# Windowed attention with a routed feed-forward layer: score mask on two engines, gathers that add, and a queue in another order

## The reference

```python
xn = layernorm(x)
q, k, v = split(xn @ qkv_w.T)            # 32 heads of 8 channels
attn = q @ k.T * 8 ** -0.5
m = where(i - 8 <= j < i + 8, (8 - abs(i - j) / 2) / 8, 0)
attn = softmax(where(m != 0, attn * m, -inf))
s = (attn @ v) @ proj_w.T + proj_b
logits = xn @ router_w                   # 8 experts
e, score = argmax(logits), sigmoid(max(logits))
h = silu(score * xn @ gate_w[e]) * (score * xn @ up_w[e])
ffn = h @ down_w[e] + (silu(xn @ sgate_w) * (xn @ sup_w)) @ sdown_w
out = x + s * silu(ffn)
```

## Time and profile before

| | |
|---|---|
| median of 3 runs | 641.51 us |
| lowest and highest | 639.12, 642.87 us |
| profiled execution, its own time | 641.16 us |
| its span, first to last instruction | 639.3 us |
| mean granted TensorE clock | 0.97 |

### The profile page before, as it was taken

How to read it: one execution, slowest core, us unless ns; L and a number is a source line. 1 busy time by engine, 2 the same in 40 slices (tenths; PEclk the granted TensorE clock), 3 DMA queues, 4 the chain that set the end, 5 groups by cost and what they waited for, 6 DMA issues and landing times. The chain is left out here.

```text
span 639.3 us, 10599 instructions
## 1 busy us (share of the span) xinstructions
PE 562.8 (88%) x3358; PEld 484.0 (76%) x3358; DVE 404.0 (63%) x853; ACT 308.1 (48%) x762; POOL 186.8 (29%) x160
## 2 busy tenths in 40 slices
PE   2879999969879999999999999999886868789865
PEld 1657888858757899898999898898775756677754
DVE  6655746886755455455455455456688888886773
ACT  1374654557773544543544634546454543635332
POOL 6000101147861011010010110014645545532230
PEclk9899999979998999999999999999989899989997
DMA  9415532112326667666567576443133333330110
GB/s 294 133 62 190 177 122 61 57 44 96 111 87 178 174 166 223 196 184 195 165 189 223 167 218 185 134 133 107 51 98 110 102 106 105 113 109 20 43 35 23
DMA packets 107370, 82.89 MB, mean 130 GB/s; under 512 B 42292, under 2 KB 104756, under 8 KB 107316
## 3 DMA queue, kind: packets, MB, share of 16 engines
q1 hardware_dynamic: 98628, 68.72, 36.6%
q0 software_dynamic: 3072, 8.39, 4.1%
q10 hardware_dynamic: 5616, 5.11, 2.3%
HBM read 59.12 MB, written 23.07 MB: 129 GB/s over the span
## 5 line engine op out<-in xcount | busy, mean ns | idle before, releaser
L425 POOL TENSOR_TENSOR Sx<-Sx,mx 128x752 f32<-128x752 f32 x64 | 93.7, 1464 | 414.9 <-DVE mx L725 414.8
L941 PE MATMUL psV<-VB,PTs 128*128 128x132 f32 x1024 | 137.3, 288 | 43.3 <-DMA VB<-v_dram 19.0
L941 PEld LDWEIGHTS psV<-VB,PTs 128*128 128x128 f32 x1024 | 130.1, 197 | 50.8 <-issue 50.0
L468 ACT ACTIVATE Or<-psV 32x128 f32<-32x128 f32 x256 | 68.5, 268 | 151.4 <-DVE rs L755 148.9
L916 PE MATMUL psS<-kBD,qBD 128*128 128x188 f32 x512 | 104.9, 329 | 0.0
L916 PEld LDWEIGHTS psS<-kBD,qBD 128*128 128x128 f32 x512 | 87.9, 195 | 10.8 <-issue 2.0
L747 DVE STREAM_TRANSPOSE PTs<-Sx 128x512 f32<-128x512 f32 x128 | 82.9, 685 | 1.0 <-ACT Sx L498 1.0
L991 PE MATMUL psM<-xT,EB 128*128 128x128 f32 x624 | 76.4, 276 | 0.0
L718 DVE TENSOR_TENSOR Sx<-psS,cst 128x752 f32<-128x752 f32 x64 | 59.7, 933 | 26.3 <-PE psS L916 26.2
L991 PEld LDWEIGHTS psM<-xT,EB 128*128 128x128 f32 x624 | 73.9, 192 | 2.1 <-ACT qBD L487 1.3
L732 DVE SCALAR_TENSOR_TENSOR ea<-et,psM 128x256 f32<-128x256 f32 x39 | 16.4, 421 | 76.3 <-PE psM L991 47.2
(11 more groups left out here) (107 smaller groups left out, 690.6 us busy)
## 6 DMA issues: line engine op xcount, KB each, us to landing
EB<-in_L_ffn_gate_w SPq DMA_DIRECT2D x39, 256.0 KB, 3.0
EB<-in_L_ffn_up_w SPq DMA_DIRECT2D x39, 256.0 KB, 3.5
EB<-in_L_ffn_down_w SPq DMA_DIRECT2D x39, 256.0 KB, 3.1
VB<-v_dram SPq DMA_DIRECT2D x256, 32.0 KB
stage<-xs_dram SPq DMA_DIRECT2D x39, 128.0 KB, 2.2
ys_dram<-yb ACTq DMA_DIRECT2D x39, 128.0 KB, 3.1
xs_dram<-blank SPq DMA_DIRECT2D x9, 512.0 KB, 3.1
v_dram<-vS SPq DMA_DIRECT2D x8, 512.0 KB, 3.0
```

The source lines that it names most:

```text
L425: nc.gpsimd.tensor_tensor(s, s, mx[n % 3][:, :].unsqueeze(2).broadcast_to([P, 2 * G, KW]), ALU.subtract).then_inc(a_sub, 1)
L468: return nc.scalar.activation(dst, src, ACT.Copy)
L941: last = mm(psV[:, j, at:at + HS * VW], PTs[n % 2][:, k, j, i, :], VB[n % 2][:, i, k, :, VW * j:VW * j + VW], start=k == 0, stop=k == 1)
```

## The change

Three things are changed together.

1. **The mask.** In steps 0 to 7 and 18 to 63 (`masked_late`) TensorE no longer writes the mask into PSUM. The constant `band` (12 x 47 fp32 values per partition, 288 KB in all) holds the mask, and a new GpSimd operation `banded(n)` adds it to `Sx` in place, after weigh and before largest, which waits for it. In these steps VectorE's `largest(n)` moves behind `flipped(n-1)`. Steps 8 to 17 keep the order and the matmuls of before. TensorE's wait for the bf16 constants moves from step 0 to step 8.
2. **The gathers.** `combine` is gone. The indirect transfers add the expert rows straight into the shared expert's rows (`compute_op=ALU.add`). Gather(c) is issued one step before its silu, after subtract, once the shared rows are there; ScalarE's silu waits for the transfers and, from chunk 3, for the buffer `Y` to be free.
3. **SyncE's order.** For units 9 to 63 `spread_v(n-1)` stands first in step n, ahead of stores, loads, fills and the wait for the scatters.

```diff
@@ constants
+    c[:, C_BAND:C_STAY] = np.tile(c[:, C_MASK:].reshape(P, 3, 1, 2 * KW), (1, 1, KC, 1)).reshape(P, 12 * KW)
+def masked_late(n):
+    return n < BATCH or n >= E0
@@ SyncE
             for n in range(LAST + 1):
+                if BATCH < n - 1 < U:
+                    spread_v(n - 1)
                 for c in result_at(n - 1):
                     store(c)
...
-                if 0 <= n - 1 < U:
+                if 0 <= n - 1 <= BATCH:
                     spread_v(n - 1)
@@ GpSimd
+            def banded(n):
+                pool.wait_ge(a_mul, n + 1)
+                s = Sx[n % 3][:, :, :].rearrange("p (m r) k -> p m r k", r=HS)[:, :, :, 0:KW]
+                kind = 2 * KC * mask_kind(n)
+                nc.gpsimd.tensor_tensor(s, s, band[:, kind:kind + 2 * KC, :].unsqueeze(2).broadcast_to([P, 2 * KC, HS, KW]),
+                                        ALU.add).then_inc(a_add, 1)
             def gather(c):
-                b = c % 3
                 if c == 0:
                     for k in range(3):
                         pool.wait_ge(b_st[k], 16 * len(range(k, NX, 3)))
-                if c >= 3:
-                    pool.wait_ge(d_w, c - 2)
+                pool.wait_ge(f_sh, c + 1)
                 for k in range(CT):
                     t = c * CT + k
-                    pool.indirect_dma_start(Y[b][:, k * C:(k + 1) * C], None, ys_dram,
-                                            bass.IndirectOffsetOnAxis(ap=slot[:, t:t + 1], axis=0)).then_inc(d_y[b], 16)
-            def combine(c):
-                b = c % 3
-                z = shared_rows(c * CT).rearrange("p t c -> p (t c)")
-                pool.wait_ge(d_y[b], 16 * CT * (c // 3 + 1))
-                pool.wait_ge(f_sh, c + 1)
-                nc.gpsimd.tensor_tensor(z, Y[b], z, ALU.add).then_inc(d_z, 1)
+                    pool.indirect_dma_start(shared_rows(c * CT)[:, k, :], None, ys_dram,
+                                            bass.IndirectOffsetOnAxis(ap=slot[:, t:t + 1], axis=0),
+                                            compute_op=ALU.add).then_inc(d_y[c % 3], 16)
             for n in range(LAST + 1):
-                for c in silu_at(n):
-                    combine(c)
                 if n < U:
+                    if masked_late(n):
+                        banded(n)
                     subtract(n)
...
-                if n == C_STEP:
-                    for c in range(3):
-                        gather(c)
-                for c in silu_at(n - 1):
-                    if c + 3 < NC:
-                        gather(c + 3)
+                for c in silu_at(n + 1):
+                    gather(c)
@@ ScalarE, silu
-                act.wait_ge(d_z, c + 1)
+                act.wait_ge(d_y[c % 3], 16 * CT * (c // 3 + 1))
+                if c >= 3:
+                    act.wait_ge(d_w, c - 2)
@@ VectorE
             def largest(n):
-                dve.wait_ge(a_mul, n + 1)
+                if masked_late(n):
+                    dve.wait_ge(a_add, len([k for k in range(n + 1) if masked_late(k)]))
+                else:
+                    dve.wait_ge(a_mul, n + 1)
...
                     weigh(n)
-                    largest(n)
+                    if not masked_late(n):
+                        largest(n)
...
                     flipped(n - 1)
+                if n < U and masked_late(n):
+                    largest(n)
@@ TensorE, scores
+                late = masked_late(n)
-                if n == 0:
+                if n == BATCH:
                     pe.wait_ge(s_cast, 2)
...
-                    mm(psS[:, j, 0:BW], identb[:, :], maskb[:, kind:kind + 2, :, :].rearrange("p i r k -> p (i r k)"),
-                       start=True, stop=False)
+                    if not late:
+                        mm(psS[:, j, 0:BW], identb[:, :], maskb[:, kind:kind + 2, :, :].rearrange("p i r k -> p (i r k)"),
+                           start=True, stop=False)
...
-                                  kBD[h % 2][:, j, :, k * QB:k * QB + KW], start=False, stop=i == 1)
+                                  kBD[h % 2][:, j, :, k * QB:k * QB + KW], start=late, stop=late or i == 1)
```

More of the change, by code:

```diff
@@ L66 @@
 C_HEAD = C_BIAS + C
-C_STAY = C_HEAD + HS
+C_BAND = C_HEAD + HS
+C_STAY = C_BAND + 12 * KW
 C_TRI, C_ONE = C_STAY, C_STAY + P
@@ L216, in build @@
         ident = cst[:, C_ID:C_ID + P]
+        band = cst[:, C_BAND:C_BAND + 12 * KW].rearrange("p (m k) -> p m k", k=KW)
         mw = cst[:, C_M:C_M + KW]
@@ L240, in build @@
         m_full = [sem(f"m_full{i}") for i in range(MB)]
-        a_qk, a_S, a_mul, a_max, a_sub, a_exp, a_PT, a_V, a_PV, a_O, a_rec, a_nrm, a_OT, a_s = (
-            sem("a_" + n) for n in ("qk", "S", "mul", "max", "sub", "exp", "PT", "V", "PV", "O", "rec", "nrm", "OT", "s"))
+        a_qk, a_S, a_mul, a_add, a_max, a_sub, a_exp, a_PT, a_V, a_PV, a_O, a_rec, a_nrm, a_OT, a_s = (
+            sem("a_" + n) for n in ("qk", "S", "mul", "add", "max", "sub", "exp", "PT", "V", "PV", "O", "rec", "nrm", "OT", "s"))
         x_v, x_vd = ([sem(f"x_{n}{i}") for i in range(2)] for n in ("v", "vd"))
@@ L248, in build @@
         d_y, d_x, d_st = ([sem(f"d_{n}{i}") for i in range(3)] for n in ("y", "x", "st"))
-        d_z, d_t, d_w, d_g, d_o = (sem("d_" + n) for n in ("z", "t", "w", "g", "o"))
+        d_t, d_w, d_g, d_o = (sem("d_" + n) for n in ("t", "w", "g", "o"))
         x_tiles = x.rearrange("(t p) c -> p t c", p=P)
```

## The result

The kernel after takes **646.58 us** (median of 6 runs, 644.66 to 647.92) beside 641.92 us (639.12 to 642.87) for the kernel before in the same comparison: a ratio of 1.008, interval 1.0052 to 1.0107. It is slower, by a little more than a measurement of this kernel can tell from no change. The prediction said 637.4 us. The time lies inside its stated range (628 to 648 us), near the upper end, but the forecast was a gain and the result is a loss, and 9.2 us are to be explained. The profiled execution took 647.14 us by its own time, with a span of 645.3 us.

The account below looks back on a forecast made before the run. TensorE was taken to bound the early steps and the full stretch, VectorE's own order the late ones. From 641.16 us, -2.4 - 6.3 - 3.7 - 0.3 - 5.4 + 7.8 + 6.5 = -3.8 gave 637.4, range 628 to 648.

Parts of the forecast that it names:

- Gathers that add: Steps 44, 48 and 52: silu waits for later-issued gathers, o_out and divide stall; 3 x 2.6 = +7.8 us.
- rival 2: Late, slower gathers hold ScalarE's queue at silu; every step with a chunk pays; 648 to 657 us, chance 0.20.
- The add on GpSimd: Mask add takes 1.80 us; largest waits 0.68 us more per step, paid where VectorE is the bound.
- the short steps: Steps 55 to 63 and tail: nine waits of 0.68, less 0.5, plus 0.9 for shared rows; +6.5 us.
- Combine's removal: Steps 42 to 54: VectorE no longer stopped, -15.5 us; with 13 x 0.78 of new waits, -5.4.
- The TensorE-bound steps: Steps 19 to 38: two mask matmuls fewer, 0.31 us a step; 6.3 us gained.
- step 18: Values' transfers first on SyncE end weighted(16)'s wait for a late transfer; -3.7 us.
- Up to weigh(8): Steps 0 to 7: mask matmuls removed while TensorE is the bound; 2.4 us gained.
- the late waits for VB: Other waits for VB, 19.0 us in all, lie beside VectorE's loop; removing them gains nothing.
- The bounds for being wrong: Wrong if the 8.37 us interval falls below 7.6 or exceeds 8.4, or TensorE's full stretch doesn't shrink by 6 us.

Follow-up runs that it names:

- e11: The changed kernel with its gathers as plain writes over the shared rows instead of adding transfers: 634.88 us, ratio 0.9902.
- e2: The kernel before with only the gathers that add, all masks on TensorE and SyncE's order as before: 645.96 us, ratio 1.008.
- e3: The kernel before with only SyncE's new order, gathers, combine and masks as before: 635.62 us, ratio 0.9927.

## Why the prediction was wrong, and where it was right

**The failed step is the term "Gathers that add", 3 x 2.6 = +7.8 us.** "What an accumulating transfer costs no row shows. [...] I take 0.3 more, since the plain gather is the nearest row." An accumulating transfer was taken for a plain one that lands 0.3 us later. Measured, silu starts 1.7 us later than the sum had it, and the three stalls are 12.2 us. Two things in the term were too small:

- the landing: 3.9 us in the median, 1.1 more than the plain one's 2.8, not 0.3. In step 48 silu starts 4.2 us after the second issue (495.11 to 499.34), where the sum had 3.1;
- the issue: the working took the 0.95 us and the distance of 1.28 from a plain gather's row. It is 1.55 and 1.85, so the second gather leaves 0.57 later. The bounds "no later" and "twice its 2.8" were set for the landing alone; that adding could cost GpSimd's own time was not asked.

The stalls measured, as idle time above that of a step without one, are 4.07 us in step 44 (5.30 before divide less 1.23), 4.22 in step 48 (6.08 less 1.86) and 3.93 in step 52, 12.2 us for 7.8. With plain transfers, in e11, they are 8.2. What the adding costs in all comes out in e11 too: 11.7 us, more than the whole 9.2 by which the forecast was off. 8.3 us of it lie in steps 42 to 54, which are 3.3 us longer than before in e11; predicted were 2.4.

**A stall that no term held** is that of step 53, 1.89 us. It is not the adding transfer's: in e11 it is 2.07 us. GpSimd and ScalarE of after, steps 52 and 53:

```profile
544.54 1.91 POOL L451 DMA_INDIRECT xnT<-ys_dram,slot  x1 [4.62 <-ACT xnT L472]
...
550.94 0.63 ACT L558 ACTIVATE EB<-xnT 128x512 f32<-128x512 f32 x1 [5.95 <-DMA xnT<-ys_dram,slot]
```

Chunk 12's gather waits 4.62 us for its shared rows, which ScalarE copies out (L472) in the same step 52, behind silu, the q and k copies and o_out; in e11 it waits 3.50. So silu starts 11.0 us after subtract's end (at 539.93) instead of 6.2. Steps 45 and 49 have the same k copies behind silu and no such wait, and they don't stall. The prediction had this wait in steps 61 and 62 only.

**How the 9.2 us of steps 42 to 54** (+11.6 for +2.4) come together: 4.4 from the three stalls, 1.9 from step 53, 2.6 from longer waits before largest (below), and 0.3 from what is left. The other stretches are off by -1.4 and +2.0 us, which nearly cancel.

The prediction's **rival 2** (0.20) had the mechanism that was missed: the transfer holds ScalarE's queue at silu with o_out behind it, slower from about 2 us of lateness, near 648. Silu was 2.0 us later than with a plain transfer (6.2 for 4.2), the time 646.58. But rival 2 let every step with a chunk pay, 5 + 4 us more, and the ordinary steps (43, 45, 49, 51) paid nothing: 7.58 to 7.59. The adding's later silu made the three stalls 4.4 us longer; the rest came from waits that rival 2 did not have, so the nearness of its 648 is partly luck. The argument against it ("mostly a fixed time") speaks of the size of a transfer and says nothing of what adding does to it.

**The add on GpSimd** was sized well: 1.65 us in the ordinary step and 1.76 in the mean, for 1.80; the wait 0.56 for 0.68. From the figure in the section "Elementwise — side-by-side cycle accounting" of "GPSIMD Engine Reference" in the Trainium skill (4,497 ns for 2,048 elements) an estimate of 1.65 us had been worked out. The trace agrees: the median of the 54 adds is 1.66. Missed was that the wait grows where a gather stands right in front. GpSimd's timeline of after, step 46:

```profile
479.03 1.93 POOL L451 DMA_INDIRECT xnT<-ys_dram,slot  x1 [0.30 <-issue]
480.46 2.17 POOL L435 TENSOR_TENSOR Sx<-Sx,cst 128x752 f32<-128x752 f32 x1
```

The add then takes 2.17 us instead of 1.65, and largest waits 1.06 to 1.08 us in steps 42, 44, 46, 50 and 52. In e11, with the shorter issue, the wait is 0.56 in steps 44, 46, 50 and 52, and 0.92 in step 42. In steps 53 and 54, where the gather in front had waited for its shared rows, it is 1.21 and 1.53. In steps 42 to 54 the waits come to 11.4 us, where 13 of 0.68 were predicted, 8.8. In front of steps 61 and 62 the gather waits for its shared rows too and stands ahead of the add. GpSimd's timeline at step 61's end:

```profile
613.63 1.83 POOL L451 DMA_INDIRECT xnT<-ys_dram,slot  x1 [1.04 <-ACT xnT L472]
615.77 1.55 POOL L451 DMA_INDIRECT xnT<-ys_dram,slot  x1 [0.30 <-issue]
616.75 2.25 POOL L435 TENSOR_TENSOR Sx<-Sx,cst 128x752 f32<-128x752 f32 x1
```

Largest waits 1.74 us in step 61 and 2.92 in step 62, together 3.5 above the ordinary 0.56 each, where the sum had 0.9. This is more than the last stretch's miss, 8.5 for 6.5. Intervals 55, 58 and 59 are longer by 0.50 to 0.53, as the short steps were said to be. Interval 60 is longer by 1.27: 0.56 is the wait for the add, and weigh(61) then waits 0.85 us for TensorE where it waited 0.29.

**Combine's removal** gave about what was forecast. For steps 42 to 54 the measured +11.6 less the four stalls (14.1) and the waits leaves 11.6 - 14.1 - 11.4 = -13.9; predicted were -15.5 and the 13 x 0.1 for divide, -14.2. The 15.5 was too much by about 1.1: it counts as combine's a divide of 1.73 us that stands at 168 us, before any combine, and after has one of 1.66 there too. e2 has the gain without the add: 7.04 for 8.37. The group of result's line in after:

```profile
L812 DVE SCALAR_TENSOR_TENSOR X<-xnT,X 128x512 f32<-128x512 f32 x14 | 9.6, 683 | 0.1
```

**The TensorE-bound steps** (intervals 20 to 38) gave 6.2 us for 6.3. From weigh(8) to weigh(20), with **step 18** and also step 19, it was 3.8 for 3.7. Up to weigh(8) it was 3.4 for 2.4, but that is no proof of the term. Intervals 1 to 6 are shorter by 0.24 to 0.32 each, as the matmuls' 0.31 says, 1.75 us together, and interval 7 by nothing. The rest lies in the start: weigh(0) is 0.6 us earlier and interval 0 is 1.1 shorter (13.31 for 14.40), and in e11, the same program up to there, interval 0 takes 14.94. What sets the start stays open. That the late waits for VB cost nothing in steps 42 to 54 is borne out by e3 (112.57 us for 112.53); in step 57 e3 is 0.8 us shorter.

**The bounds for being wrong** hardly caught it. The interval of 8.37 us fell to 7.58, just under the 7.6 that was set, because the step was cheaper than thought (the wait 0.56 for 0.68, divide hardly later), which has nothing to do with the loss. The TensorE stretch lay within its bound. The loss came in the steps with stalls, for which "divide late in steps 44, 48 and 52" named the place but no size beyond which the forecast fails.

## What to carry to other kernels

When an operation is folded into a DMA, price it on both sides: what the issuing engine pays for each (here 0.6 us) and how much later it lands (1.1 us), and bound the two apart. Ask as well what the transfer now has to wait for before it can be issued: here the rows that it adds to, 4.6 us in one step. A transfer that replaces work done a few steps ahead must keep that lead, or its consumer must stand at the end of its queue: either edit was worth about 10 us here. And move work off the busiest engine only in the steps in which that engine is the bound; the same edit gained 10 us in TensorE's steps and lost 12 to 18 us in VectorE's.

## What the runs showed of the hardware

- An indirect DMA that adds (128 rows of 1 KB, two to a chunk) costs GpSimd 1.55 us to issue against 0.97 plain, and lands in 3.9 us against 2.8 (3.0 in e11). Its queue's packets doubled for the same 8.39 MB, from 3072 to 6144 for the whole run; in e11 they are 3072.
- A GpSimd add right behind such an issue takes 2.17 to 2.25 us instead of 1.65. The two records overlap by 0.5 us, so part of it may be the tail of the issue; which part was not separated.
- The same add keeps 1.65 us beside VectorE's transposes, and these keep 1.29 for their two.
